# Relative-position attention with the scores made twice, the second time with keys as rows

## The reference

```
attn  = (q * 16**-0.5) @ k.T                                  # N x N
attn += rel_h[..., :, None] + rel_w[..., None, :]             # q . Rh, q . Rw: one term by key row, one by key column
out   = softmax(attn, axis=-1) @ v
```

## Time and profile before

| what | us |
|---|---|
| median of three runs (lowest, highest) | 1468.78 (1464.65, 1472.25) |
| the profiled execution, its own time | 1465.66 |
| span of the profile, first to last instruction | 1463.9 |
| PE busy | 1138.0 (78%) |
| PE weight loads busy (beside PE) | 801.8 (55%) |
| DVE busy | 665.5 (45%) |
| ACT busy | 441.4 (30%) |
| POOL busy | 94.1 (6%) |

### The profile page before, as it was taken

One profiled execution on the slowest core, in us unless ns is written; L12 is line 12 of the kernel. 1 busy time (PEld: TensorE's weight loads), 2 busy tenths in 40 slices (PEclk: granted clock), 3 DMA queues, 4 the chain that ended last, 5 costly groups with the idle time before them and its releaser, 6 DMA issues. The chain is left out here.

```text
span 1463.9 us, 28380 instructions
## 1 busy us (share of the span) xinstructions
PE 1138.0 (78%) x10258; PEld 801.8 (55%) x10259; DVE 665.5 (45%) x1945; ACT 441.4 (30%) x1186; POOL 94.1 (6%) x132
## 2 busy tenths in 40 slices
PE   0888889777877979897978429993697897549993
PEld 0666467644655757574637317772373473436772
DVE  6266126722652737474847602222583374431223
ACT  2244225411431435342424103330241252112220
POOL 2000000010000000000000040003100000040004
PEclk9988788877787989797969659997797998768997
DMA  7000000020000000009300231111910000021113
GB/s 191 2 3 2 1 2 3 2 79 6 3 1 2 2 1 1 1 2 190 134 1 1 54 93 43 48 47 50 210 66 0 0 1 1 1 75 47 46 48 103
DMA packets 31965, 57.24 MB, mean 39 GB/s; under 512 B 3461, under 2 KB 28678, under 8 KB 30826
## 3 DMA queue, kind: packets, MB, share of 16 engines
q1 hardware_dynamic: 28664, 48.34, 12.2%
q0 software_dynamic: 3072, 6.30, 1.5%
q10 hardware_dynamic: 114, 1.04, 0.3%
HBM read 41.80 MB, written 13.86 MB: 38 GB/s over the span
## 5 line engine op out<-in xcount | busy, mean ns | idle before, releaser
L719 ACT ACTIVATE work<-banks,nmax 128x256 f32<-128x256 f32 (+3 forms) x528 | 198.6, 427 | 196.2 <-DVE nmax L758 195.1
L638 PE MATMUL banks<-K,Q 128*28 128x196 f32 (+5 forms) x1056 | 204.5, 359 | 18.9 <-PEq L87 18.9
L758 DVE TENSOR_REDUCE nmax<-banks 128x2 f32<-128x512 f32 (+3 forms) x264 | 153.4, 581 | 100.1 <-PE banks L663 62.6
L1318 PE MATMUL banks<-gu,sxT 96*128 x496 | 177.8, 503 | 0.8 <-ACT sxT L1353 0.6
L638 PEld LDWEIGHTS banks<-K,Q 96*128 96x128 f32 (+4 forms) x1056 | 142.7, 176 | 35.4 <-issue 23.3
L214 PE MATMUL banks<-xT,weights 96*96 96x512 f32 (+3 forms) x288 | 150.2, 682 | 9.5 <-ACT xT L426 8.8
L767 DVE COPY work<-banks 128x512 f32<-128x512 f32 (+3 forms) x264 | 149.5, 566 | 10.3 <-PE banks L674 8.9
L1379 DVE TENSOR_TENSOR h<-sg,banks 128x384 f32<-128x384 f32 x62 | 34.4, 555 | 236.4 <-ACT sg L1361 236.4
L674 PE MATMUL banks<-small,work 128*128 128x128 f32 (+2 forms) x912 | 139.7, 270 | 0.0
L1318 PEld LDWEIGHTS banks<-gu,sxT 96*128 96x128 f32 x496 | 92.8, 197 | 54.5 <-issue 7.6
L674 PEld LDWEIGHTS banks<-small,work 128*128 128x128 f32 (+2 forms) x912 | 102.1, 139 | 22.9 <-ACT work L719 7.3
(11 more groups left out here) (209 smaller groups left out, 1402.4 us busy)
## 6 DMA issues: line engine op xcount, KB each, us to landing
gu<-in_L2f_gu SPq DMA_DIRECT2D x1, 6912.0 KB, 36.8
xin<-slots_in SPq DMA_DIRECT2D x62, 96.0 KB, 1.9
slots_out<-y SPq DMA_DIRECT2D x62, 96.0 KB, 1.6
gu<-in_L3f_gu SPq DMA_DIRECT2D x1, 5184.0 KB, 31.4
dn<-in_L2f_dn SPq DMA_DIRECT2D x1, 4608.0 KB, 47.8
slots_in<-zeros SPq DMA_DIRECT2D x1, 2976.0 KB, 11.3
dn<-in_L3f_dn SPq DMA_DIRECT2D x1, 2592.0 KB, 37.4
gu<-in_L2f_gu SPq DMA_DIRECT2D x1, 2304.0 KB, 13.6
```

What stands on the lines that cost most here:

```text
L638: ins = nc.tensor.matmul(S(s)[r0:r0 + rn, hh, 0:lay.width(t)], lay.q(m, t, h, win), lay.k(m, t, h, win), start=(hh == 0 or kind != "causal ...
L719: ins = nc.scalar.activation(w.Pr[0:rows, s % 3, hh, 0:lay.width(t)], S(s)[0:rows, hh, 0:lay.width(t)], ACT.Exp, bias=w.nmax[0:rows, s % 4 ...
L758: nc.vector.tensor_reduce(w.nmax[0:rows, s % 4, :], S(s)[0:rows, :, 0:lay.width(t)], AX.X, ALU.max, negate=True).then_inc(max_ready, 1)
L1318: ins = nc.tensor.matmul(banks[:, 2 + 2 * par + n, 0:EF], w.sxT[:, par, k, :], w.gu[:, bass.ds(e, 1), k, n * EF:(n + 1) * EF].rearrange("p ...
```

## The change

The new function `attend_relative` takes the place of `attend` in L0 and L1. A unit is now an image and a pair of heads, with all its queries: 12 units per stage. The scores are made twice. The first time queries are rows, and only DVE reads them, for the negated maxima, which it writes into column 48 (head 0 of the pair) and 112 (head 1) of a tile `nmax` of 128 columns that is zero elsewhere. PE turns this tile by transposes, so that the maxima stand in partitions 48 and 112 with the queries along the row, and DVE adds the result to Q. Row 48 of the key code is now all ones, so the second product already has the maximum subtracted. It is made with keys as rows, three steps later (LAG), ACT takes its exp for both heads and all queries in one instruction, and PE multiplies this with V as it is. The transposes of the exponentials and DVE's copies of them are gone. In the products of Q and K each head contracts over its own 64 partitions (`r`), the two heads' passes alternate and go to different banks; Q has no zero halves, and the memsets for them are gone (a smaller one for `nmax` comes on POOL).

The functions not shown do the following. `turn_outputs`, `divide`, `turn_normed`, `turned_back`, `project` and `residual` do the work after the heads as before, with all 256 queries of an image at once (outputs of four heads go out of PSUM in one 128x256 copy; an image has six transposes of outputs, two divisions, four transposes back, one ACT copy of 96x512, in L0 one per window part, and eight projection passes). `relative_buffers` holds the new tiles. The layer norm `ahead` is left out in two of the four stages, where nothing reads it.

```diff
-            chain(nc.gpsimd.memset(w.Q[64:P, 0::2, :], 0.0))
+            chain(nc.gpsimd.memset(w.nmax[:, :, :, :], 0.0))
...
-            chain.free(nc.vector.memset(w.Q[0:64, 1::2, :], 0.0))
...
-        def queries_out(copy, g, half):
-
-            rows = slice(64 * half, 64 * half + 64)
-            bank, q = banks[rows, (2 + n_vjobs + g) % 4, :], w.Q[rows, 2 * g + half, :]
+        def queries_out(copy, g):
+            bank, q = banks[:, (2 + n_vjobs + g) % 4, :], w.Q[:, g, :]
...
-            for g in range(6):
+            for g in range(1, 6, 2):
                 dve.wait_ge(a_done, 2 + n_vjobs + g + 1)
-                queries_out(nc.vector.tensor_copy, g, 1).then_inc(odd_out, 1)
-            dve.wait_ge(odd_out, 6)
+                queries_out(nc.vector.tensor_copy, g).then_inc(odd_out, 1)
...
-            for a in range(2 + n_vjobs + 6):
+            for a in [*range(2 + n_vjobs), *range(2 + n_vjobs, 2 + n_vjobs + 6, 2)]:
...
-                    ins = queries_out(nc.scalar.copy, a - 2 - n_vjobs, 0)
+                    ins = queries_out(nc.scalar.copy, a - 2 - n_vjobs)
...
+def attend_relative(nc, env, w, ip, windows):
...
+        def key_columns(n):
+            if not windows:
+                return [(0, TOKENS, 0, 0), (0, TOKENS, P, TOKENS)]
+            if n == 0:
+                return [(0, WN, 0, 0), (0, WN, 98, WN)]
+            nq = WINDOW_BOX[n][1] * WINDOW_BOX[n][3]
+            return [(WINDOW_AT[n], nq, n * WN + 98 * c, 2 * WN + 60 * c + WINDOW_AT[n] - WN) for c in range(2)]
+        window_list = range(WINDOWS) if windows else range(1)
+        def s_banks(u):
+            return 0 if windows else 2 * (u % 2)
+        def st_banks(u):
+            return 0 if u >= U - 2 and u % 2 == 0 else 4
+        def st_before(u):
+            return [v for v in range(u) if st_banks(v) == st_banks(u)][-1:]
...
+            def scores(u):
+                m, g = divmod(u, HP)
+                q, k = w.Q[:, g, m * TOKENS:(m + 1) * TOKENS], w.K[:, g, m, :]
+                if u >= (1 if windows else 2):
+                    pe.wait_ge(max_ready, u if windows else u - 1)
+                for t in range(2):
+                    for hh in range(2):
+                        r = slice(64 * hh, 64 * hh + 64)
+                        ins = nc.tensor.matmul(banks[0:ck, s_banks(u) + hh, t * keys:(t + 1) * keys],
+                                               q[r, t * ck:(t + 1) * ck], k[r, 0:keys], start=True, stop=True)
+                if windows:
+                    for n in range(1, WINDOWS):
+                        nq = WINDOW_BOX[n][1] * WINDOW_BOX[n][3]
+                        for hh in range(2):
+                            r = slice(64 * hh, 64 * hh + 64)
+                            ins = nc.tensor.matmul(banks[32 * (n - 1):32 * (n - 1) + nq, 2 + hh, 0:WN],
+                                                   q[r, WINDOW_AT[n]:WINDOW_AT[n] + nq], k[r, n * WN:(n + 1) * WN],
+                                                   start=True, stop=True)
+                ins.then_inc(scores_ready, 1)
+            def turn_max(u):
+                pe.wait_ge(max_ready, u + 1)
+                pe.wait_ge(misc_read, misc.index(("max", u)))
+                at = 0
+                for t, rows in enumerate(tile_rows):
+                    ins = nc.tensor.transpose(banks[:, 7, at:at + rows], w.nmax[0:rows, u % 2, t, :], ident[0:rows, 0:rows])
+                    at += rows
+                ins.then_inc(max_turned, 1)
+            def scores_turned(u):
+                m, g = divmod(u, HP)
+                q, k = w.Q[:, g, m * TOKENS:(m + 1) * TOKENS], w.K[:, g, m, :]
+                pe.wait_ge(max_in, u + 1)
+                for v in st_before(u):
+                    pe.wait_ge(exp_ready, v + 1)
+                for n in window_list:
+                    for q0, nq, k0, at in key_columns(n):
+                        for hh in range(2):
+                            r = slice(64 * hh, 64 * hh + 64)
+                            ins = nc.tensor.matmul(banks[0:ck, st_banks(u) + hh, at:at + nq], k[r, k0:k0 + ck],
+                                                   q[r, q0:q0 + nq], start=True, stop=True)
+                ins.then_inc(st_ready, 1)
+            def weigh(G):
+                m, g = divmod(G, 3)
+                pe.wait_ge(exp_ready, 2 * G + 2)
+                if G >= 1:
+                    pe.wait_ge(O_out, G)
+                for n in window_list:
+                    for c, (q0, nq, k0, at) in enumerate(key_columns(n)):
+                        for j in range(4):
+                            u, h = 2 * G + j // 2, 4 * g + j
+                            v = w.V[0:98, m * 8 + n * 2 + c, h, :] if windows else w.V[:, m * 2 + c, h, :]
+                            ins = nc.tensor.matmul(banks[32 * j:32 * j + VW, 6, q0:q0 + nq], v,
+                                                   w.PT[0:ck, u % 3, j % 2, at:at + nq], start=(c == 0), stop=(c == 1))
+                ins.then_inc(pv_done, 1)
...
+            misc = [("max", u) for u in range(10)] + [("OM", 0), ("max", 10), ("OM", 1), ("max", 11),
+                                                      ("OT", 0), ("out", 0), ("OT", 1)]
+            for s in range(U + LAG + 1):
+                if s < U:
+                    scores(s)
+                if 1 <= s <= U:
+                    turn_max(s - 1)
+                if LAG <= s < U + LAG:
+                    scores_turned(s - LAG)
+                if s - LAG >= 2 and (s - LAG) % 2 == 0:
+                    weigh((s - LAG) // 2 - 1)
+                first = s - (HP + LAG + 1)
+                if first in (0, 1):
+                    turn_outputs(0, first)
...
+            def exponent(u):
+                act.wait_ge(st_ready, u + 1)
+                if u >= 3:
+                    act.wait_ge(pv_done, (u - 3) // 2 + 1)
+                at = st_banks(u)
+                nc.scalar.activation(w.PT[0:ck, u % 3, :, :], banks[0:ck, at:at + 2, :], ACT.Exp).then_inc(exp_ready, 1)
...
+            if windows == (ip == 0):
+                ahead = normalise_steps(nc, chain, env.ahead_s, env.ahead, other, 1e-5, True)
...
+            def maxima(u):
+                m, g = divmod(u, HP)
+                at = s_banks(u)
+                dve.wait_ge(scores_ready, u + 1)
+                if u >= 2:
+                    dve.wait_ge(max_turned, u - 1)
+                rows_of_max = slice(MAX_ROW, P, 64)
+                out = w.nmax[0:ck, u % 2, 0:2, rows_of_max].rearrange("p t s -> p s t")
+                ins = nc.vector.tensor_reduce(
+                    out, banks[0:ck, at:at + 2, 0:2 * keys].rearrange("p s (t k) -> p s t k", t=2), AX.X, ALU.max, negate=True)
+                if windows:
+                    ins = nc.vector.tensor_reduce(w.nmax[0:68, u % 2, 2, rows_of_max], banks[0:68, 2:4, 0:WN], AX.X, ALU.max,
+                                                  negate=True)
+                ins.then_inc(max_ready, 1)
+            def turned_maxima(u):
+                m, g = divmod(u, HP)
+                q, turned = w.Q[:, g, m * TOKENS:(m + 1) * TOKENS], banks[:, 7, :]
+                dve.wait_ge(max_turned, u + 1)
+                if windows:
+                    nc.vector.tensor_tensor(q[:, 0:WN], q[:, 0:WN], turned[:, 0:WN], ALU.add)
+                    pair = q[:, WN:WN + 56].rearrange("p (n q) -> p n q", n=2)
+                    nc.vector.tensor_tensor(pair, pair, turned[:, WN:WN + 64].rearrange("p (n q) -> p n q", n=2)[:, :, 0:28],
+                                            ALU.add)
+                    ins = nc.vector.tensor_tensor(q[:, WN + 56:], q[:, WN + 56:], turned[:, WN + 64:WN + 68], ALU.add)
+                else:
+                    ins = nc.vector.tensor_tensor(q, q, turned[:, 0:TOKENS], ALU.add)
+                ins.then_inc(max_in, 1)
+                dve.wait_ge(max_in, u + 1)
+                dve.sem_inc(misc_read, 1)
...
+            for s in range(U + LAG + 1):
+                if s < U:
+                    maxima(s)
+                if 1 <= s <= U:
+                    turned_maxima(s - 1)
...
+                for _ in range(0 if s < 2 else 3):
+                    if next(ahead, "done") == "done":
+                        next(behind, None)
+            for _ in ahead:
...
+            w.work = sb("work", [P, 3 * 2 * BANK])
+            w.PT = w.work[:, :].rearrange("p (u h n) -> p u h n", u=3, h=2)
...
-                w.Q = sb("Q", [P, HEADS, PN])
+                w.Q = sb("Q", [P, HEADS // 2, PN])
...
-                    attend(nc, env, w, "windows" if windows else "full", ip, None, not windows,
-                           1e-5 if windows else None, windows)
+                    attend_relative(nc, env, w, ip, windows)
...
         hot[:, r, j] = 1
         hot[:, 32 + c, j] = 1
```

More of the change, by code:

```diff
@@ L32 @@
 BANK = 512
+MAX_ROW = 48
 RSQRT_SEED = 0x5F3759DF
@@ L403, in _ @@
                 else:
-                    for m in range(PAIR):
```

(35 more changed lines are left out.)

118 lines of the change are left out of this document (added).

## The result

| | before | after |
|---|---|---|
| median (lowest, highest), 12 runs each, us | 1463.70 (1459.56, 1472.25) | 1481.84 (1468.75, 1498.66) |
| profiled execution, its own time | 1465.66 | 1488.72 |
| its span | 1463.9 | 1486.9 |
| PE busy | 1138.0 | 1149.2 |
| DVE busy | 665.5 | 595.4 |

The changed kernel is slower: ratio 1.0108, interval [1.0079, 1.0138]. The forecast was 1452, and the time lies above the range's 1480. The changed kernel's times go with the clock: 0.839 in the run of 1468.75, 0.827 in the profiled one of 1488.72, which is 6.9 us above the median, so that its stages show more than the typical loss. Ratios leave out runs over 1.5% above the fastest of their kernel, here the one of 1498.66.

What follows compares the result with a forecast made beforehand. PE was taken as close to the bound, DVE behind it. Setups -5.7, L1 -9.7 and L0 -0.9 gave -16.3: 1449.4 us from the profiled 1465.7, and 1452 with the median 3.1 higher; range 1437 to 1480.

Steps and rivals of the forecast that it cites:

- rival C: L1 and L0 attention: the row halves don't overlap, +103 us for four stages, 1555 us; chance 0.09.
- The 24 narrow passes: L0 remainder with keys as rows: 98 weight columns each, halves' loads side by side, 0.98 us per unit.
- rival E: Products of the row halves overlap, loads don't: L0's remainder pays +11.7 us a stage, 1476 us; chance 0.06.
- Exp, maxima and addition: L1, ACT and DVE: exp over 1024 elements 1.1 us, a maximum 1.22, the addition to Q 0.42.
- The setup's gain: L0 setup: DVE's memset goes and POOL's gets smaller, 4.6 us saved.
- L1's gain: L1's two attention stages: 48.3 us against 53.4 and 52.9, so -5.1 and -4.6.
- clock 1.9: L0 attention stage's sum: 1.9 us lost to the half clock, within 61.6 us.
- start 0.5: Attention stage's sum in L0: 0.5 us added for the start, the same as in L1.
- Rival D: Attention stages: TensorE falls to half clock; L1's stages about +25 us each, 1502 us; chance 0.08.
- PE has little idle time: Argument against a fall to half clock in the attention stages, beside passes using all rows in pairs.
- the change of shape: PE in the attention units: 0.095 us per change between product shapes, 0.29 us a unit in L1, 0.38 in L0.
- Rival B: Attention units: the loop between engines, not PE, sets the pace at 3.3 us; only setups gain, 1463 us; chance 0.14.

Runs made afterwards that it cites:

- x6: The kernel before, with L0's scores in steps 1 to 8 waiting for the exp of the unit before: 1494.51 us, ratio 1.0195 to the kernel before.
- x3: The changed kernel plus two products nobody reads in the first three steps of each L0 stage: 1472.45 us, ratio 1.0009 to the kernel before.
- x5: The changed kernel with unread filling products at L0's first three steps and its other gaps: 1464.72 us, ratio 0.9990 to the kernel before.
- x1: The new attention in L1 alone, L0 with the old one, zero padding included: 1463.31 us, ratio 0.9949 to the kernel before.
- x2: The new attention in L0 alone, L1 with the old one: 1497.25 us, ratio 1.0181 to the kernel before.
- x4: The changed kernel, L0's second scores leaving out the remainders of windows 1 to 3: 1463.52 us, ratio 0.9935 to the kernel before.
- x7: The changed kernel, window 0's scores in L0 waiting only for window 0's maxima of the unit before: 1476.35 us, ratio 1.0090 to the kernel before.
- x9d: New attention in L1 only, with L1's second scores directly behind the first ones: 1463.05 us, ratio 0.9955 to the kernel before.
- x10d: New attention in L1 only, plus two filling products before each group of 32-row products in the projection stages: 1471.81 us, ratio 1.0008 to the kernel before.

## Why the prediction was wrong

*Right.* The halves of the rows do overlap at the full rate: in the new trace two passes of a pair start 0.007 us apart and pairs 0.166 (196 columns) and 0.216 (256) apart, so rival C is refuted. The 24 narrow passes take about 1.0 us a unit (pairs 0.087 apart, booked 0.082): their loads lie side by side, so rival E is refuted. Exp, maxima and addition came as booked. The setup's gain of 4.8 was booked as 4.6, and L1's gain had the right sign.

*The step that failed* is the term "clock 1.9" in L0's sum, together with "start 0.5". It carried the old stage's start, where three banks of scores keep PE fed and the clock is up within 3.8 us, over to an order in which PE waits for DVE before the second, third and fourth unit. I had priced waits only for PE's steady state. In the changed kernel PE idles 0.9 of the 3.8 us in 83.4 to 87.2, stands at 0.50 for 37.4 and 16 us of the two stages, and falls back to it for the last 28.8 us of the first. At 0.50 a unit without weighing takes 6.29 us (94.65 to 100.94), at 1.00 3.41 (119.23 to 122.64). x6 shows that waits alone hold the clock down while they last, and x3 and x5 that products put into the idle time bring it up. Why the first stage stayed down for 25 us more, with PE busy throughout, no run shows.

*Rival D* was this mechanism, but at 0.08, and put into L1 because I multiplied by L1's unit. L1's scores alternate between two pairs of banks, and its clock read 0.94 and 0.96, better than before. My argument against D, "PE has little idle time", was an average over a stage; the clock was lost in the first units, where it is not true. The profile of before had the warning in the earlier trace rows: one projection ends in 18.4 us at 0.50, so that the attention begins at 1.2 GHz, as the earlier trace rows also show.

The Trainium skill, TensorE: Matmul & The Clock Gate, A second HAM failure mode: psum-queue depth-cycling, says that short idle spells of PE between groups of products, in a kernel that cycles through PSUM banks, can make its clock go up and down. The trace agrees as far as short spells go (0.97 to 1.6 us beside 37.4 us at 0.50). It differs in that the spells here come from a single pair of banks, and that the clock stayed down instead of going up and down.

*Mis-sized: the change of shape.* Booked at 0.095 us. Two units of L1 take 431.73-425.89 = 5.84 us; without changes my prices give 2x(0.86+0.86+0.22)+0.86 = 4.74, so six changes took 1.10, or 0.18 each, if all of the rest is put down to them. In L0 two units take 127.27-119.23 = 8.04 for 7.62 booked. That is 12x0.265 = 3.2 us of a stage in L1, which took 50.5 for 48.3, so that 1.0 of the rest was booked too high; and 2.5 in L0. The rest of L0's 5.2 us at full clock (66.8 against 61.6) is the loop: in x5 filling and waits take 1.7, 1.4 and 1.4 us ahead of the second, third and fourth unit. With the 2.5 that is 7.0, so that 1.8 was booked too high elsewhere. Rival B was thus true of L0's first four units, and of no others.

*The sum again.* L1 -5.3 (booked -9.7), the stretches with the setups -5.8 (booked -5.7: -4.8 in L0, -1.0 in L1, where the setup itself went from 6.7 to 5.0 us), L0 +37.8 (booked -0.9) of which x5 gives back all but 9.5, the first projection -2.4 (booked at nothing), all else -1.3. L0 gains nothing at any clock here: what the transposes cost before goes to the narrow passes and the loop. The version that beats both kernels is x1, 0.9949.

*Open.* How long the clock stays down varies: 37.4 and 16 us in the changed kernel, about 16 in both stages of x2, 18 and 17 in x4, 15 and 21 in x7. What decides between 16 and 37 us was not found. It came once in six stages with the new passes whole and unfilled, so x4's and x6's two stages each can't exclude a share of the narrow or the 64-row passes in it. Nor is it told apart whether x3's and x5's products raise the clock by taking PE's idle time away or by being dense work of 128 rows: x7 took 1.4 us of idle time from each start, added no work, and had its clock in one of its stages no sooner than the changed kernel in its second one, in the other 1 us sooner. That the 0.18 us are the change of shape itself rests on the timeline alone, and x9d speaks against it: six changes fewer should have saved 1.1 us a stage and saved 0.4 and 0.2.

## What to carry to other kernels

When an order is rebuilt, walk its first units, before the pipeline has filled, as carefully as its steady state: look up which buffers are single there, and what TensorE does while it waits. If the stretch ahead leaves it at 1.2 GHz, short waits there can cost far more than they last: the 3.5 us of each L0 stage cost this program some 14 us with what the clock lost (x3). A layer whose shape makes narrow passes should be timed apart from its sister before both are changed. Filling products pay where PE would idle (x3, x5) and cost as much as they bring where it is busy (x10d).

## What was unexpected of the hardware

- TensorE, after the idle spells at 0.50, stayed there although it was then busy without a gap: for 25.1 us in 88.4 to 113.5. In nine other starts it was at 1.00 between 3.5 and 10.3 us after a wait. Conversely it fell right behind a single wait of 0.87 us at 137.4.
- The same products in the same order got 0.63 in one stage and 0.83 in the other. The changed kernel's times, without the slowest, spread over 1.4%, before over 0.9%; but x2's, with the same L0, over 0.8%, so that the spread is no sure sign.
- Passes of 64 rows in two halves run fully side by side in float32 (pairs start 0.007 us apart). A step among products of different shapes took about 0.18 us longer than the products' own prices, where the change from 128-row scores to weighing in the earlier trace rows had shown 0.095; whether it is the change was not shown.
- A memset on POOL held a tiny DVE operation for its whole length, more than once. Before, DVE had two in a row, 2.71 us and 2.73 us, beside POOL's memsets of 2.66 (the zero padding) and 2.71 us. In the changed kernel the first has 0.79 us beside the memset of `nmax` of 0.74, and the second is as long as before. Timelines of DVE before and after:

```profile
16.63 2.73 DVE L109 TENSOR_SCALAR norm_a<-norm_v 128x4 int32<-128x4 int32 x1
```

```profile
14.09 0.79 DVE L107 TENSOR_SCALAR norm_v<-norm_mean_var 128x4 f32<-128x4 f32 x1
14.91 2.74 DVE L110 TENSOR_SCALAR norm_a<-norm_v 128x4 int32<-128x4 int32 x1
```
